# An LSTM over 512 steps on one core: scales of the x blocks worked out by GpSimd, and the kernel's first products in another order

## The reference

```
xW = einsum('ntd,dg->ntg', x, Wx) + b        # Wx: 512 x 2048
step:  a = xW[t] + h @ Wh                    # Wh: 512 x 2048
       i, f, o = sigmoid(a[:, :3*512])  (512 each);  g = tanh(a[:, 3*512:])
       c = f * c + i * g;   h = o * tanh(c)  # h0 = cond_1024, c0 = 0
out = x + hs
```

## Time and profile before

| what | value |
|---|---|
| median of the runs | 2542.74 us |
| the profiled execution, its own time | 2543.45 us |
| its span, first to last instruction | 2541.4 us |
| mean granted TensorE clock | 0.999 of full |
| TensorE matmuls busy | 2525.8 us |
| VectorE busy | 1938.7 us (76%) |
| ScalarE busy | 1554.5 us (61%) |
| GpSimd busy | 160.8 us (6%) |
| chain that ended last, TensorE's share | 98% |

### The profile page before, as it was taken

How to read it: one execution, slowest core, us unless ns; L and a number is a source line. 1 busy time by engine, 2 the same in 40 slices (tenths; PEclk the granted TensorE clock), 3 DMA queues, 4 the chain that set the end, 5 groups by cost and what they waited for, 6 DMA issues and landing times.

```text
span 2541.4 us, 161390 instructions
## 1 busy us (share of the span) xinstructions
PE 2525.8 (99%) x67268; PEld 1801.8 (71%) x67268; DVE 1938.7 (76%) x8091; ACT 1554.5 (61%) x5895; POOL 160.8 (6%) x264
## 2 busy tenths in 40 slices
PE   9999999999999999999999999999999999999998
PEld 3677777777777777777777777777777777777775
DVE  7777777777777777777777777777777777777776
ACT  8666666666666666666666666666666666666664
POOL 1000000000000000000000000000000000000000
PEclk9999999999999999999999999999999999999999
DMA  7111111111112111111121111111111121111111
GB/s 238 43 37 37 41 45 37 37 41 45 37 37 41 45 37 37 41 45 37 37 41 45 37 37 41 45 37 37 41 45 37 37 42 45 37 37 43 43 33 35
DMA packets 58364, 114.24 MB, mean 45 GB/s; under 512 B 6496, under 2 KB 7136, under 8 KB 57312
## 3 DMA queue, kind: packets, MB, share of 16 engines
q0 software_dynamic: 19008, 35.53, 9.9%
q1 hardware_dynamic: 39248, 78.30, 9.1%
q10 hardware_dynamic: 80, 0.03, 0.0%
HBM read 79.23 MB, written 33.55 MB: 44 GB/s over the span
## 4 chain that ended last, share of the span: by engine, by line
PE 98%; DVE 1%; DMA 1%; ACT 0%; SPq 0%; issue 0%; DVEq 0%; ACTq 0%
PE Z L389 72%; PE run L389 19%; PE extra L389 6%; DMA h_T<-in_h_cols 1%; DVE wx_lo L932 0%; ACT tanh_c L644 0%; DVE h_hi L994 0%; SPq L309 0%; DVE gc L1011 0%; DVE igfc L1005 0%; ACT act L633 0%; ACT wx_hi L658 0%; DVE gc L1020 0%; DVE igfc L1007 0%; DVE hT_hi L999 0%
## 5 line engine op out<-in xcount | busy, mean ns | idle before, releaser
L389 PE MATMUL Z<-wh_hi,hT_hi 128*32 128x512 f16 x8176 | 795.9, 379 | 7.0 <-DVE hT_hi L999 6.9
L389 PE MATMUL Z<-wh_lo,hT_hi 128*32 128x512 f16 x8176 | 796.0, 379 | 0.0
L633 ACT ACTIVATE act<-Z 128x128 f32<-128x128 f32 x1024 | 287.2, 281 | 569.7 <-PE Z L389 569.7
L389 PE MATMUL Z<-wh_hi,hT_lo 128*32 128x512 f16 x8176 | 529.8, 379 | 0.0
L644 ACT ACTIVATE tanh_c<-gc 128x64 f32<-128x64 f32 x1024 | 262.8, 257 | 311.3 <-DVE gc L1020 248.7
L389 PE MATMUL run<-wx_hi,x_hi 128*32 128x256 f16 x6048 | 427.3, 273 | 1.2 <-DVE x_lo L799 1.2
L389 PE MATMUL Z<-wx_hi,x_hi 128*32 128x256 f16 x6048 | 427.4, 273 | 0.2 <-DVE wx_lo L932 0.2
L389 PE MATMUL Z<-wx_lo,x_hi 128*32 128x256 f16 x6048 | 427.3, 273 | 0.0
L389 PE MATMUL Z<-wx_hi,x_lo 128*32 128x256 f16 x6048 | 427.3, 273 | 0.0
L389 PE MATMUL run<-wx_lo,x_hi 128*32 128x256 f16 x6048 | 427.3, 273 | 0.0
L389 PE MATMUL run<-wx_hi,x_lo 128*32 128x256 f16 x6048 | 427.3, 273 | 0.0
(11 more groups left out here) (121 smaller groups left out, 3923.3 us busy)
## 6 DMA issues: line engine op xcount, KB each, us to landing
y<-in_x_rows POOLq DMA_DIRECT2D x127, 256.0 KB, 4.0
out_y<-y SPq DMA_DIRECT2D x127, 256.0 KB, 2.0
x_T<-in_x_cols SPq DMA_DIRECT2D x126, 256.0 KB, 2.7
wx_raw<-in_Wx SPq DMA_DIRECT2D x4, 1024.0 KB, 12.8
wh_raw<-in_Wh SPq DMA_DIRECT2D x4, 1024.0 KB, 13.5
t<-in_Wx SPq DMA_DIRECT2D x3, 512.0 KB, 18.5
t<-in_Wx POOLq DMA_DIRECT2D x3, 512.0 KB, 5.8
x_raw<-in_x_cols SPq DMA_DIRECT2D x2, 256.0 KB, 6.2
```

The source lines that it names most:

```text
L389: return nc.tensor.matmul(out, lhsT, rhs, start=False, stop=last, skip_group_check=True)
L633: nc.scalar.activation(half_gates(act, a)[:, 0:2], half_gates(Z[s], a)[:, 0:2], ACT.Sigmoid, scale=scale).then_inc(gates_done, 1)
```

## The change

The scales of a block move from VectorE to GpSimd. VectorE keeps only the masking of the exponent field, which now comes ahead of the maximum over the partitions instead of behind it, and four operations of GpSimd behind the maximum write the five scales: negate, the z scale, one addition for four scales and one operation for the fifth. The semaphore scales_done counts two per block. In the same way Wx's scale and the tables go to GpSimd.

TensorE: h0 is loaded ahead of Wh. The first bank's list ends with two bias parts for banks 4 and 5 instead of bank 4 whole; banks 4 to 7 are finished behind steps 1 to 4 (before: 5 to 7 behind steps 1 to 3, bank 4 ahead of step 1), with the bias parts of banks 6 and 7 behind steps 2 and 3.

Weights: T4 for cp = 0 is made in a place of its own (`t1[:, 1]`), so that it need not wait, and before the sums of |Wh|; VectorE sums half of two chunks of Wh instead of half of one. T1 for cp = 1 goes into the raw weights, and its load waits until TensorE and VectorE are through with them. Low cuts of Wx stand up to one step sooner in VectorE's list, T1's high cut one step later in ScalarE's.

```diff
@@ sync
             load_raw_x(1)
+            sp.dma_start(h_T[:, :, :].rearrange("p ch b -> p (ch b)"), h0_cols).then_inc(h0_loaded, 16)
             load_weights(sp, wh_raw, Wh, wh_loaded, range(NCH))
-            sp.dma_start(h_T[:, :, :].rearrange("p ch b -> p (ch b)"), h0_cols).then_inc(h0_loaded, 16)
...
-            sp.dma_start(t1[:, 1], Wx[1][:, HG:]).then_inc(t1_loaded, 16)
             sp.dma_start(bias_d[:, :], bias_rows[:, HW:]).then_inc(bias_d_loaded, 16)
+            sp.wait_ge(raw_done, 2)
+            sp.wait_ge(t4_made, 1)
+            sp.wait_ge(wx_lo_cut, CUT[W_NAMED["B21"], 0] + 1)
+            sp.dma_start(w_form(W_NAMED["T1"], 1), Wx[1][:, HG:]).then_inc(t1_loaded, 16)
@@ tensor
             def rest_of_raw(s):
-                bias_part(s)
...
-            for s in range(2, TB + 1):
+            for s in range(2, TB):
+                bias_part(s)
                 rest_of_raw(s)
+            bias_part(TB)
+            bias_part(TB + 1)
...
-                        if isinstance(t, int) and t < TB:
-                            rest_of_raw(TB + t)
+                        if isinstance(t, int) and t <= TB:
+                            rest_of_raw(TB + t - 1)
+                        if isinstance(t, int) and 2 <= t < TB:
+                            bias_part(TB + t)
@@ scalar
             sum_of_wh(1, G)
-            sum_of_wh(2, G)
+            cut_wx_hi(0, "T3")
+            sum_of_wh(2, HG)
             sum_of_wh(3, HG)
-            cut_wx_hi(0, "T3", "B22", "T4")
+            cut_wx_hi(0, "B22", "T4")
...
                 if s == 1:
                     scale_raw(2)
+                    sc.wait_ge(row_scale_done, 2)
+                    cut_wx_hi(1, "B11")
                     sum_of_x(2, 0, 1)
                     scale_raw(3)
-                    sc.wait_ge(row_scale_done, 2)
-                    cut_wx_hi(1, "B11")
...
                 if s == 3:
-                    cut_wx_hi(1, "B21", "T1")
+                    cut_wx_hi(1, "B21")
                     scale_raw(6)
             def last_cuts(s):
                 if s == 0:
-                    cut_wx_hi(1, "T3")
                     scale_raw(7)
+                    cut_wx_hi(1, "T1", "T3")
+                if s == 1:
                     cut_wx_hi(1, "B22")
@@ vector
                     if first(n) and s == 1:
-                        weight_scale(1)
-                        scale_tables()
-                        scale_block(2, 0)
+                        cut_wx_lo(0, "T4")
+                        field_of_sum(2, 0)
+                        cut_wx_lo(1, "B11")
                     if first(n) and s == 2:
-                        cut_wx_lo(0, "T4")
-                        cut_wx_lo(1, "B11")
+                        cut_wx_lo(1, "T2")
                     if first(n) and s == 3:
-                        cut_wx_lo(1, "T2")
+                        cut_wx_lo(1, "B21")
                     if first(n - 1):
                         if s == 0:
-                            cut_wx_lo(1, "B21", "T1")
+                            cut_wx_lo(1, "T1", "T3")
                         if s == 1:
-                            cut_wx_lo(1, "T3", "B22")
+                            cut_wx_lo(1, "B22")
...
-                    if s == 3 and within(n + 3, NB):
-                        negate_field(n + 3)
...
-                            scale_of_z(n + 3)
-                            scales_of_block(n + 3, 1 - r)
@@ gpsimd
             def share_xmax(n, r):
-                pool.wait_ge(xmax_done, nth_block(n))
+                pool.wait_ge(xfield_done, nth_block(n))
+                pool.sem_inc(xmax_seen, 1)
+                nc.gpsimd.partition_all_reduce(xmax_all[:, r:r + 1], xfield[:, r:r + 1].bitcast(F32), P,
+                                               bass.bass_isa.ReduceOp.max).then_inc(xmax_shared, 1)
+            def scale_block(n, r):
+                pool.wait_ge(xmax_shared, nth_block(n))
...
+                nc.gpsimd.tensor_scalar(xfield_n[:, 0:1], xmax_all[:, r:r + 1].bitcast(I32), float(LOW_FIELD << MANT), -1.0,
+                                        ALU.max, ALU.mult).then_inc(xfield_n_done, 1)
...
+                nc.gpsimd.tensor_scalar(zs[:, 0:1], xfield_n[:, 0:1], zs_of_x[:, :], zs_of_h[:, :],
+                                        ALU.add, ALU.min).then_inc(zs_done, 1)
...
+                nc.gpsimd.tensor_scalar(scales[:, r, 0:4], scale_add[:, :], zs[:, 0:1], None,
+                                        ALU.add).then_inc(scales_done, 1)
+                nc.gpsimd.tensor_scalar(scales[:, r, 4:5], zs[:, 0:1], -1.0, float((2 * EXP_ONE) << MANT),
+                                        ALU.mult, ALU.add).then_inc(scales_done, 1)
...
             add_w(t1[:, 0], t2_loaded, Wx[1][:, 0:HG], t2_added)
-            share_wmax(1)
+            wx_scale()
+            scale_tables()
             share_xmax(2, 0)
+            scale_block(2, 0)
             def block(i, n, r):
                 if within(n + 3, NB):
                     share_xmax(n + 3, 1 - r)
+                    scale_block(n + 3, 1 - r)
                 if within(n + 1, NB):
                     add_x(i, n, r)
```

More of the change, by code:

```diff
@@ L122, in lstm_residual @@
         xfield_n = sb("xfield_n", [P, 2], I32)
[L123 removed]
+        zs = sb("zs", [P, 1])
         scales = sb("scales", [P, 2, 5], I32)
@@ L177, in lstm_residual @@
         w_scale_done = sem("w_scale_done")
+        pool_seen = sem("pool_seen")
+        wx_field_done = sem("wx_field_done")
+        wx_field_c_done = sem("wx_field_c_done")
+        wx_scale_done = sem("wx_scale_done")
         tables_done = sem("tables_done")
@@ L266, in w_form @@
                 return t3[:, 0]
+            if cp == 0 and k == W_NAMED["T4"]:
+                return t1[:, 1]
+            if cp == 1 and k == W_NAMED["T1"]:
+                return w_block(1, 0)[:, 0]
             return (w_block(0, 0), w_block(1, 0), w_block(1, 1), w_block(1, 0), t1, w_block(0, 1), t3)[k][:, cp]
@@ L810, in field_of_sum @@
             def field_of_sum(n, r):
[L811 to L812 removed]
+                v.wait_ge(xmax_done, nth_block(n))
+                if started(nth_block(n - 2)):
+                    v.wait_ge(xmax_shared, nth_block(n - 2))
+                nc.vector.tensor_scalar(xfield[:, r:r + 1], xmax[:, r:r + 1].bitcast(I32), 255 << MANT, None,
                                         ALU.bitwise_and).then_inc(xfield_done, 1)
[L815 to L829, removed]
[L830 to L837 removed]
             def set_h_scale(n, r):
@@ L975, in prepare @@
                 cut_wx_lo(0, "B21", "T1", "T2")
-                sum_of_last_wh()
                 make_t4()
+                sum_of_half_wh(2)
+                sum_of_half_wh(3)
                 largest_weight(0)
@@ L990, in prepare @@
                 largest_weight(1)
+                v.wait_ge(wmax_done, 2)
+                nc.vector.tensor_scalar(wfield[:, 1:2], wmax[:, 1:2].bitcast(I32), 255 << MANT, None,
+                                        ALU.bitwise_and).then_inc(wx_field_done, 1)
             def high_part_of_h(t, a):
@@ L1113, in block @@
                     if s == 3:
-                        if within(n + 3, NB):
-                            scale_of_z(n + 3)
                         if taken(2 * n + 4):
                             cut_x_lo(2 * n + 4, r, 0)
-                        if within(n + 3, NB):
-                            scales_of_block(n + 3, 1 - r)
             prepare()
@@ new lines, in share_wmax, with wx_scale @@
+            def share_wmax():
+                pool.wait_ge(wmax_done, 1)
+                nc.gpsimd.partition_all_reduce(wmax_all[:, 0:1], wmax[:, 0:1], P,
+                                               bass.bass_isa.ReduceOp.max).then_inc(wmax_shared, 1)
+            def wx_scale():
+                pool.wait_ge(wx_field_done, 1)
+                nc.gpsimd.partition_all_reduce(wmax_all[:, 1:2], wfield[:, 1:2].bitcast(F32), P,
+                                               bass.bass_isa.ReduceOp.max).then_inc(wmax_shared, 1)
+                pool.wait_ge(wmax_shared, 2)
+                nc.gpsimd.tensor_scalar(wfield_c[:, 1:2], wmax_all[:, 1:2].bitcast(I32), float(LOW_FIELD << MANT), None,
+                                        ALU.max).then_inc(wx_field_c_done, 1)
+                pool.wait_ge(wx_field_c_done, 1)
+                nc.gpsimd.tensor_scalar(w_scale[:, 3:4], wfield_c[:, 1:2], -1.0,
+                                        float((2 * EXP_ONE + TOP_W) << MANT), ALU.mult, ALU.add).then_inc(wx_scale_done, 1)
@@ new lines, in scale_tables @@
+            def scale_tables():
+                pool.wait_ge(w_scale_done, 1)
+                pool.wait_ge(wx_scale_done, 1)
+                pool.wait_ge(row_scale_done, 2)
+                nc.gpsimd.tensor_scalar(zs_of_x[:, :], w_scale[:, 3:4], float((EXP_ONE + TOP_X) << MANT), None,
+                                        ALU.add).then_inc(tables_done, 1)
```

(5 more changed lines are left out.)

58 lines of the change are left out of this document (18 added, 40 removed).

## The result

The changed kernel takes 4195.08 us (median of 4 runs, 4188.75 to 4197.26); beside it the kernel before took 2542.76. The ratio is 1.6493, 95% interval 1.6475 to 1.6512: 65% slower, where 0.14% faster was forecast. The profiled execution took 4188.75 us, its span 4187.1.

A forecast was written before the change was run, and what follows sets the result against it. TensorE, busy 99%, leaves only the first 78 us to win: the start at 78.18 becomes 74.72, steady blocks unchanged. The median 2542.74 less 3.46 gives 2539.3 us (0.14% faster), range 2537.8 to 2543.0.

The forecast's parts named there:

- The steady blocks: The blocks behind the head: four GpSimd operations at 0.3 us each, hidden with 1.05 us to spare; VectorE's relief worth nothing.
- The first use of GpSimd's arithmetic is slow: Rival, 8%: the first scale operations and a maximum need 8.1 instead of 5.8 us; 2541.6 us, to 2543 if more.
- Scales late in every block: Rival, 3%: GpSimd's scales come late in each block; needs over 1.0 us per operation, then 12 us per tenth.
- low clock: TensorE at 0.50 near 61 us, costing 1.69 us, expected to go; rival that it stays: 12%, 2541.0 us.
- GpSimd holds VectorE: Rival, slower, 12%: the moved operations block VectorE in each block; two of 0.15 give 2546.7 us, two of 0.35 2596.
- the head: The first 78 us, up to the start at 78.18: the only place to win, with 8.8 us of waiting or low clock.
- the two waits: TensorE's idle times of 1.17 and 1.04 us before the starts at 58.20 and 60.07, both expected to go.
- step 3: TensorE's recurrent step in the first 78 us: forecast to start at 47.77 and end at 50.36.
- step 8: TensorE's step that started at 78.18: forecast to start at 74.72, 3.46 us sooner, with 0.72 idle.
- h0's gain: TensorE's wait of 0.94 at 21.23 goes, but Wx's last chunk leaves the first step only 0.31 us sooner.
- the removed bias part: One part fewer ahead of TensorE's second step; a 0.72 us stall for Wh's low cut eats its gain, leaving 0.43.
- the copy: Copy of the first block of sums to its bank: forecast to end at 61.87, making TensorE wait 1.15 us.

The follow-up runs named there:

- one_copy: The kernel before with one spare tensor_copy of one column on GpSimd behind each maximum of x: 2542.58 us, ratio 0.9999.
- four_memsets: The kernel before with four spare one-column memsets on GpSimd behind each maximum of x: 2542.70 us, ratio 0.9999.
- one_scalar_op: The kernel before with one spare one-column tensor_scalar on GpSimd behind each maximum of x: 2682.87 us, ratio 1.0555.
- no_maximum: The changed kernel with GpSimd's maxima over the partitions for x and Wx replaced by one more small operation: 2548.22 us, ratio 1.0021.
- scales_only: The kernel before with only GpSimd's part of the change (scales, tables, Wx's scale, field ahead of the maximum), old orders kept: 4184.03 us, ratio 1.6446.
- spare_maximum: The changed kernel with one more, unneeded maximum over the partitions on GpSimd at the end of each block's list: 3536.00 us, ratio 1.3904.
- spare_and_sooner: The changed kernel with a spare maximum ending each block's GpSimd list and VectorE's field operation one step sooner: 2798.23 us, ratio 1.1005.
- order_only: The kernel before with TensorE's new order alone: 2542.73 us, ratio 0.9999.
- reorder_a: The changed kernel with all scale arithmetic back on VectorE and its low cuts in the old order: 2542.05 us, ratio 0.9997.
- run 659: Not a run's label but a time difference: the run meant is spare_maximum, 659 us shorter than the changed kernel, at 3536.00 us.

## Why the prediction was wrong

**The step that failed** is "The steady blocks", in its price for GpSimd: "I take 0.3 each and keep 0.10 to 0.8", "0.4 to 3.2 us for the four", "So it is hidden at both ends." The size of the operations was right (0.19 to 0.40 each, 1.7 for the four). What was missing is a term of another kind: two changes of kind on GpSimd a block, 6.1 and 7.4 us, on the chain from field to scales. They made TensorE wait 10.8 us a block and run at half clock behind it, 13.3 us lost in each, 65% where 0.14% faster was forecast. The trace before has no scalar operation of GpSimd, so its rows could not bound what comes with the first one; I bounded the operation by its neighbours (a memset, a maximum) and took the bound for one of the change. The DMA descriptors stood beside the maxima without a gap, which looked like evidence that kinds mix freely; one_copy and four_memsets show that this holds for copies and memsets too, and one_scalar_op that it does not hold for tensor_scalar.

**The rivals.** "The first use of GpSimd's arithmetic is slow" was nearest: the first one had 8.52 us of "issue" ahead of it in no_maximum. But I saw it as paid once, and gave it 8%. The row that I had it from, 1.30 us for the first maximum, need not be a first use: in scales_only the same maximum takes 0.38, where VectorE's cut starts only behind it.

```profile
23.68 0.38 POOL L1122 PARTITION_ALL_REDUCE wmax_all<-wmax  x1 [23.11 <-DVE wmax L876]
```

```profile
23.82 1.28 DVE L918 SCALAR_TENSOR_TENSOR wx_lo<-t,w_scale,wx_hi 128x1024 f16<-128x1024 f32 x1 [0.28 <-ACT wx_hi L661]
```

That bears out the other reading of the row, that GpSimd waited for a VectorE operation already under way. spare_maximum shows it too: the real maxima start while VectorE's low x runs (2020.65 to 2021.34) and take 0.62 on the mean, the spare ones 0.38. "Scales late in every block" (3%) is the path the loss takes, with the price that I gave it, 12 us for each tenth of a us: 11 us late make some 1320, against 1353.1 of TensorE's waits. The low clock is not in that price, and I had it need "over 1.0 us per operation". "GpSimd holds VectorE" is refuted by no_maximum. None had the alternation.

**"The field before the maximum"** I had treated as harmless. It was not: the maximum now waits for VectorE's field in the fourth step instead of ScalarE's sum in the third. spare_and_sooner gets back 738 us against spare_maximum by that step alone. It is a mistake only together with the changes of kind: in no_maximum the field has the same place and the block is 19.53 us.

**The clock.** The prediction knew a low clock as 1.69 us, once. With a wait of 10.8 us in each block it comes in each block, 2.5 us a time, some 300 us of the loss. That it would go from the head with the two waits was right for the order of TensorE: the clock is 1.00 in order_only, whose waits there are 0.98 at most.

**The head was right up to step 3.** There the changed kernel starts within 0.16 us of the forecast, but for the products with h0 (20.80 for 20.29, taken up by the wait for Wx). The same working put step 8 at 77.1 in reorder_a and at 77.6 in order_only, where it came at 76.75 and 77.54. That h0's gain is taken by Wx's last chunk, the removed bias part by the low cut of Wh (0.60 for 0.72), and the low clock mostly by the copy, the runs confirm. The steps behind step 3 wait for the late scales in the changed kernel, so the forecast of 3.46 us was not tested whole: it rests on GpSimd doing the arithmetic without a gap, and reorder_a, with the arithmetic on VectorE, gives 1.43. By the same working the difference is VectorE's longer list; no run takes it off. One reading of the old trace was short: TensorE also waits at 66.55 (0.38), 70.47 (0.15) and 72.59 (0.63), inside the 8.8 us but not in my list. The last of them stays in reorder_a (0.63 ahead of step 7), where I had forecast none.

## What to carry to other kernels

Before an operation goes to GpSimd, ask whether that kind already runs there beside its present ones; if the trace doesn't show the pair, price two changes per alternation, 6 to 8 us each for this pair, and look for them as "issue" ahead of the operation. If they can't be avoided, group the kinds (the four small operations in a row pay once), or run a spare operation of the needed kind in idle time. A bound from neighbouring rows bounds the operation, not what has to happen before it.

## What I had not expected of the hardware

The change falls due when the queue reaches it, and here that is behind the wait for the field: in the changed kernel 6.1 us start only with the field at 2033.87, though GpSimd had been idle since 2017.8. The program agrees: in the block's list the wait for the field stands ahead of the extra instruction, and an increment of xmax_seen stands between the wait and the maximum. Ahead of the run's first maximum (23.38) the extra instruction comes first and the wait is part of the maximum, and that one starts 0.13 us behind its input (VectorE's wmax, over at 23.25) without a gap. Whether the change to the maximum would be hidden in each block with the wait placed so, no run tries; it is the first thing that I would try next.

The DMA descriptors of y take 1.05 us on the mean in the kernels that alternate, 0.91 in no_maximum and 0.88 in those without a scalar operation on GpSimd; the reason is open. And a spare operation of 0.38 us, 128 times, made a run 659 us faster.
